# Flamingo layer on one core: transposes of y and h, and of two of four key blocks, by VectorE turns and DMA moves instead of TensorE

## The reference

```python
x = x + tanh(g_xattn) * xattn(layernorm(x), ctx, ctx, Wq, Wk, Wv, Wo, bo, g)
x = x + tanh(g_ffn) * ffn(layernorm(x), A, B, Wr)

# xattn, per batch; 8 heads of 64; the softmax of k runs over the 1024 positions, that of q over a head's 64 channels
qh = softmax(Wq @ q, over channels) * 64**-0.5
kh = softmax(Wk @ k, over positions)
context = einsum('hdn,hen->hde', kh, Wv @ v)
out = Wo @ einsum('hde,hdn->hen', context, qh) + bo
out = out / norm(out, over channels) * g * sqrt(128)

# ffn: 64 experts of rank 16, the top 16 of each token
gates = softmax(top16(x @ Wr.T)), 0 for the others
out = ((x @ A.T) * gates) @ B.T * 2
```

## Time and profile before

| | |
|---|---|
| median of 3 runs | 960.5 us (959.32 to 960.53) |
| profiled execution | 959.67 us, span of its instructions 957.9 us |
| TensorE busy | 932.2 us, 97% of the span |
| VectorE / ScalarE / GpSimd busy | 704.0 / 492.2 / 469.5 us |
| mean granted TensorE clock | 0.994 |
| stage one, rounds | context product to context product about 33 us, 16 batches |
| stage two, rounds | 24.8 us, 16 batches |

### The profile page before, as it was taken

How to read it: one execution, slowest core, us unless ns; L and a number is a source line. 1 busy time by engine, 2 the same in 40 slices (tenths; PEclk the granted TensorE clock), 3 DMA queues, 4 the chain that set the end, 5 groups by cost and what they waited for, 6 DMA issues and landing times.

```text
span 957.9 us, 16074 instructions
## 1 busy us (share of the span) xinstructions
PE 932.2 (97%) x5084; PEld 800.5 (84%) x5084; DVE 704.0 (73%) x1532; ACT 492.2 (51%) x974; POOL 469.5 (49%) x323
## 2 busy tenths in 40 slices
PE   7899999999999999999999799999999999999998
PEld 5687887888888888888888699999999999999986
DVE  6888888888888888888888857766666666666521
ACT  4687786678768767876787634222222222222100
POOL 3775657678777877785787824222222111111100
PEclk9999999999999999999999999999999999999999
DMA  4226231231323113311312853121111111111001
GB/s 153 89 66 249 93 104 49 89 133 66 109 91 133 66 68 132 109 68 66 131 45 88 300 199 128 67 67 67 66 67 67 66 66 66 66 66 45 23 23 44
DMA packets 24805, 88.31 MB, mean 92 GB/s; under 512 B 3264, under 2 KB 3264, under 8 KB 24768
## 3 DMA queue, kind: packets, MB, share of 16 engines
q1 hardware_dynamic: 19296, 67.91, 19.9%
q0 software_dynamic: 5184, 19.40, 6.1%
q10 hardware_dynamic: 288, 0.52, 0.2%
HBM read 71.04 MB, written 16.78 MB: 92 GB/s over the span
## 4 chain that ended last, share of the span: by engine, by line
PE 81%; DVE 10%; issue 5%; ACT 1%; POOL 1%; DMA 1%; DVEq 0%; ACTq 0%; POOLq 0%
PE ps L61 22%; PE ps L63 22%; PE ps L62 22%; PE ps L1307 6%; PE ps L1298 4%; DVE qT_lo L909 3%; PE ps L1288 2%; PE ps L1402 1%; PE ps L1373 1%; DVE mt L933 1%; DVE ekT_lo L916 1%; DVE qmax L895 1%; DVE bn L831 1%; DVE kmax L889 1%; DVE qsum L900 1%
## 5 line engine op out<-in xcount | busy, mean ns | idle before, releaser
L471 POOL TENSOR_TENSOR rb<-u_in,rb 128x1024 f32<-128x1024 f32 x14 | 33.7, 2408 | 255.4 <-DVE rb L885 255.4
L400 POOL TENSOR_TENSOR qe<-qe,qrec 128x1024 f32<-128x1024 f32 x64 | 121.2, 1903 | 47.1 <-DVE qrec L903 47.1
L61 PE MATMUL ps<-aT_hi,yT_hi 128*128 128x448 f32 (+2 forms) x384 | 128.4, 334 | 5.4 <-issue 5.4
L63 PE MATMUL ps<-aT_lo,yT_hi 128*128 128x448 f32 (+2 forms) x384 | 126.6, 330 | 0.0
L62 PE MATMUL ps<-aT_hi,yT_lo 128*128 128x448 f32 (+2 forms) x384 | 126.5, 330 | 0.0
L909 DVE TENSOR_TENSOR qT_lo<-ps,qT_hi 128x512 fp32r<-128x512 f32 x128 | 82.4, 686 | 49.0 <-ACT qT_hi L628 48.5
L393 POOL TENSOR_TENSOR qhalf<-qe 128x512 f32<-128x512 f32 x64 | 82.2, 1284 | 64.8 <-ACT qe L620 61.8
L61 PE MATMUL ps<-bT_hi,hT_hi 128*128 128x512 f32 x256 | 102.6, 401 | 0.0
L63 PE MATMUL ps<-bT_lo,hT_hi 128*128 128x512 f32 x256 | 100.0, 391 | 0.0
L62 PE MATMUL ps<-bT_hi,hT_lo 128*128 128x512 f32 x256 | 99.8, 390 | 0.0
L700 ACT ACTIVATE hT_hi<-ps 128x512 fp32r<-128x512 f32 x32 | 19.1, 597 | 143.8 <-PE ps L1402 143.8
(11 more groups left out here) (155 smaller groups left out, 2397.5 us busy)
## 6 DMA issues: line engine op xcount, KB each, us to landing
x_in<-in_x SPq DMA_DIRECT2D x16, 512.0 KB, 4.4
ctx_in<-in_ctx SPq DMA_DIRECT2D x16, 512.0 KB, 4.9
ctxT_in<-in_ctxT SPq DMA_DIRECT2D x16, 512.0 KB, 3.4
ctxT_hi<-in_ctxT POOLq DMA_DIRECT2D x16, 512.0 KB, 3.8
u_scratch<-osb SPq DMA_DIRECT2D x16, 512.0 KB, 3.8
out<-res SPq DMA_DIRECT2D x16, 512.0 KB, 2.8
x<-in_x SPq DMA_DIRECT2D x15, 512.0 KB, 4.0
u_in<-u_scratch SPq DMA_DIRECT2D x14, 512.0 KB, 3.2
```

The source lines that it names most:

```text
L61: nc.tensor.matmul(psum, whi, mhi, start=start, stop=False)
L63: return nc.tensor.matmul(psum, whi, mlo, start=False, stop=stop)
L400: nc.gpsimd.tensor_tensor(v, v, w, ALU.mult).then_inc(q_norm, 1)
```

## The change

Where it no longer uses TensorE, a transpose of a 128 x 1024 block takes three steps: VectorE transposes each 32 x 32 square in place (`turn_k`, `turn_y`, `turn_h`), SyncE issues 16 DMAs of 32 partitions x 256 columns that put strips of 32 columns into the partitions that they belong to (`move_turned`), and the high and low parts are made from the moved copy in SBUF (`hi_moved_*`, `lo_moved_*`).

- Stage two: y of batches 2 to 15 and h of all batches. `tr_h` is gone, `down` runs as one piece behind `up` of the next batch. A and B are laid out on the host so that rows fit the strips. y of batches 0 and 1 stays with TensorE.
- Stage one: key blocks 0 and 1. Blocks 2 and 3 stay with TensorE. `exp_k` of blocks 0 and 1 writes in strip order. Block 0 is turned in place, block 1 into a buffer of its own. The low part is made by GpSimd (`lo_moved_k`).
- The fourth query pair is normalised by ScalarE in 16 pieces of 64 columns (`normalise_q`) instead of by GpSimd.
- GpSimd's order: `normalise(b-1, 2)` goes ahead of `halve(b-1, 3)`, `halve(b, 1)` ahead of `lo_ctx(b+1, ...)`, the two `lo_moved_k` are added.
- SyncE: the loads of A go into the loop, one a round, instead of eight in a row; the moves stand behind the load of ctx and ahead of that of x.

```diff
+        def move_turned(queue, dst, src, s, slot=None):
+            for a in range(P // 32):
+                for q in range(P // 32):
+                    rows, cols = slice(32 * a, 32 * a + 32), slice(256 * q, 256 * q + 256)
+                    queue.dma_start(dst[32 * q:32 * q + 32, 256 * a:256 * a + 256],
+                                    src[rows, cols] if slot is None else src[rows, slot, cols]).then_inc(s, 16)
...
# SyncE
+            def move_k(b, j):
+                if j == 0 and started(b):
+                    wait_apart(sp, sp_turns, (kc_mm, b))
+                wait_apart(sp, sp_turns, (k_turned, turned_before(b, j) + 1))
...
                     load(ctx_in[:, :], ctx, b + 1, ctx_loaded)
+                    for j in TURNED:
+                        move_k(b, j)
...
+                if not isinstance(i, int) or b <= NB - 2:
+                    sp.wait_ge(y_turned, b)
+                    move_turned(sp, y_raw, y[(j + 2) % 2], y_moved)
                 if not isinstance(i, int) or b <= NB - 4:
-                    sp.wait_ge(y_T, 2 * b + 4)
+                    sp.wait_ge(y_moved, MOVED * b)
                     load_u(b + 3, j % 2)
+                sp.wait_ge(h_turned, b + 1)
+                move_turned(sp, h_raw, hg, h_moved)
# GpSimd
+            def lo_moved_k(b, j):
+                pool.wait_ge(k_hi, 8 * b + 2 * j + 2)
...
+                nc.gpsimd.tensor_tensor(lo, ekT_raw[j][:, :], hi.bitcast(f32), ALU.subtract).then_inc(k_lo_pool, 1)
# ScalarE
+            def hi_moved_k(b, j):
+                act.wait_ge(k_moved[j], MOVED * (b + 1))
+                nc.scalar.activation(..., ekT_raw[j][:, :], ACT.Copy).then_inc(k_hi, 2)
+            def normalise_q(b, p):
+                act.wait_ge(q_rec, 4 * b + p + 1)
+                for n in range(2 * H):
+                    v = qe[:, p, DH * n:DH * n + DH]
+                    last = nc.scalar.activation(v, v, ACT.Copy, scale=qrec[:, p, n:n + 1])
...
                     hi_kc(b - 1)
+                    normalise_q(b - 1, 3)
...
-                    hi_k(b, 0)
+                    hi_moved_k(b, 0)
+                if tail and head:
+                    hi_q(b - 1, 2)
+                if head:
                     exp_k(b, 2)
                     exp_q(b, 1)
-                if tail and head:
-                    hi_q(b - 1, 2)
# VectorE
+            def turn_k(b, j):
+                dve.wait_ge(k_exp, 4 * b + j + 1)
+                nc.vector.transpose(ek[:, 0, :] if j == 0 else ek_turned[:, :], ek[:, j % 2, :]).then_inc(k_turned, 1)
...
                     sum_q(b - 1, 2)
+                if head:
+                    turn_k(b, 0)
...
                     max_k(b, 2)
-                    lo_k(b, 0)
+                    turn_k(b, 1)
# stage two on VectorE
                     result(b - 2, ...)
+                    lo_moved_h(b - 1)
                     part_u(b + 2)
+                    turn_y(b + 1, j % 2)
                 route(b)
-                lo_h(b - 1, 1)
                     norm_u(b + 2)
                     gated(b, p)
-                    lo_y(b + 1)
-                lo_h(b, 0)
+                turn_h(b)
+                    lo_moved_y(b + 1)
                     stats2(b + 2, ...)
# TensorE, stage two
                 up(b, 0)
-                    tr_h(b - 1, 1)
+                    sum_u(b + 2)
                 up(b, 1)
                 up(b, 2)
-                    sum_u(b + 2)
-                    tr_y(b + 1, j % 2)
-                down(b - 1, 0)
-                tr_h(b, 0)
-                down(b - 1, 1)
+                down(b - 1)
```

More of the change, by code:

```diff
@@ L198, in flamingo_layer @@
             sem("k_mm"), sem("k_max"), sem("k_exp"), sem("k_T"), sem("k_hi"), sem("k_lo"), sem("k_rec"))
+        k_turned, k_moved, k_lo_pool = sem("k_turned"), [sem(f"k_moved{j}") for j in range(CH)], sem("k_lo_pool")
         q_mm, q_max, q_shift, q_exp, q_half, q_sum, q_rec, q_norm, q_T, q_hi, q_lo = (
@@ L293, in _ @@
             sp.wait_ge(wq_low, 1)
-            for t in range(DC):
-                sp.dma_start(a_raw[:, t, :], AT[t]).then_inc(a_loaded, 16)
-            with sp.Fori(2, NB - 2) as b:
+            with sp.Fori(2, 2 + DC) as b:
+                sp.dma_start(a_raw[:, bass.ds(b - 2, 1), :].rearrange("p o n -> p (o n)"),
+                             AT[bass.ds(b - 2, 1)].rearrange("o p n -> (o p) n")).then_inc(a_loaded, 16)
+                body(b, head=True, tail=True, ahead=True)
+            with sp.Fori(2 + DC, NB - 2) as b:
                 body(b, head=True, tail=True, ahead=True)
@@ L534, in _ @@
             pool.sem_inc(a_low, 1)
-            with pool.Fori(SPLIT, SPLIT + DC) as b:
+            cast_a(0)
+            with pool.Fori(SPLIT, SPLIT + DC - 1) as b:
                 body(b, head=True, tail=True, ahead=True, split=True)
+            body(SPLIT + DC - 1, head=True, tail=True, ahead=True, split=True)
             with pool.Fori(SPLIT + DC, NB - 2) as b:
@@ L1392, in up @@
                 last.then_inc(h_mm, 1)
-            def tr_h(b, g):
-                pe.wait_ge(hg_done, 3 * b + 2 + g)
-                if g == 1 or started(b):
-                    pe.wait_ge(h_lo, 2 * b + g)
-                else:
-                    pe.wait_ge(o_out, 2 * NB)
-                for n in range(4):
-                    w = (4 * g + n) * P
-                    last = nc.tensor.transpose(psG[:, n * P:n * P + P], hg[:, w:w + P], ident[:, :])
-                last.then_inc(h_T, 1)
@@ L1405, in down @@
-            def down(b, part_):
-                pe.wait_ge(h_lo, 2 * b + part_ + 1)
-                for g in range(2):
-                    if part_ == 0 and started(b):
-                        pe.wait_ge(res_done, 2 * b - 2 + g + 1)
-                    elif part_ == 0 and g == 0:
-                        pe.wait_ge(o_out, 2 * NB)
-                    v = slice(512 * g, 512 * g + 512)
-                    for m in range(KC // 2 * part_, KC // 2 * (part_ + 1)):
-                        if not started(b) and g == 0:
-                            wait_weight(pe, m)
-                        last = three_pass(psF[:, g, :], hT[0][:, m, :], hT[1][:, m, :], bT[0][:, m, v],
-                                          bT[1][:, m, v], m == 0, m == KC - 1)
-                    if part_ == 1:
-                        last.then_inc(f_mm, 1)
+            def down(b):
+                hi, lo = hT_last if isinstance(b, int) and b == NB - 1 else hT
+                first = isinstance(b, int) and b == 0
+                pe.wait_ge(h_lo, 2 * b + 2)
+                for strips in (range(KC // 2), range(KC // 2, KC)) if first else (range(KC),):
+                    for g in range(2):
+                        if first:
+                            pe.wait_ge(o_out, 2 * NB)
+                        else:
+                            pe.wait_ge(res_done, 2 * b - 2 + g + 1)
+                        v = slice(512 * g, 512 * g + 512)
+                        for m in strips:
+                            if first and g == 0:
+                                wait_weight(pe, m)
+                            last = three_pass(psF[:, g, :], hi[:, m, :], lo[:, m, :], bT[0][:, m, v],
+                                              bT[1][:, m, v], m == 0, m == KC - 1)
+                        if strips[-1] == KC - 1:
+                            last.then_inc(f_mm, 1)
@@ L1448, in body @@
                     mm_k(b, 2)
-                    tr_k(b, 0, next(turn))
                 if tail and head:
+                    tr_q(b - 1, 2, next(turn))
                     output(b - 1, 0, range(CH // 2))
@@ L1458, in body @@
                         up(0, 0)
-                    tr_q(b - 1, 2, next(turn))
-                    if not head:
+                        tr_q(b - 1, 2, next(turn))
                         output(b - 1, 0, range(CH))
@@ L1464, in body @@
                     mm_q(b, 2)
-                    tr_k(b, 1, next(turn))
                 if tail and head:
@@ L1550, in folded, with strips @@
         return w.reshape(-1, p, w.shape[1]).transpose(1, 0, 2).reshape(p, -1)
+    def strips(w):
+        return w.reshape(p // 32, -1, 32, w.shape[1]).transpose(1, 0, 2, 3).reshape(-1, p, w.shape[1])
     laid = {
```

208 lines of the change are left out of this document (136 added, 72 removed).

## The result

| | before | after |
|---|---|---|
| median | 960.5 us | 1152.0 us (4 runs, 1149.2 to 1158.1) |
| ratio | | 1.200, 95% interval 1.196 to 1.205 |
| span of the profiled execution | 957.9 us | 1149.8 us |
| TensorE busy, share of the span | 932.2 us, 97% | 961.5 us, 84% |
| mean granted TensorE clock | 0.994 | 0.926 |

What follows compares the result with a forecast made beforehand. TensorE was taken to bound both stages, VectorE close behind in stage one. Profiled 959.7 us + 44 (stage one) + 4 (first batch) + 1 (entry) + 1.3 (end) - 26.8 (stage two) = 983, forecast 984 us; range 934 to 1012.

Steps and rivals of the forecast that it cites:

- What bounds the kernel: Both stages: TensorE sets the time, busy 32.69 of 32.90 us in stage one with VectorE close behind, 24.77 in stage two.
- the chain that was named: Stage one: VectorE's turn of key block 1, SyncE's move, ScalarE's copy delay key block 2's transposes; +2.9 us a round.
- chain (b): Stage two, SyncE alone: move y, reload, move h, plus 5.9 us between; 21.9 us, fitting under TensorE's 22.96.
- X: Time of one move, first issue until all 16 DMAs landed: 8.0 us, ends 6.3 and 9.9.
- steps 1 to 5: Stage one, from VectorE's key block 0 turn to TensorE's key block 2 transposes: round 35.8 instead of 32.9, some +44 us.
- rival C: Stage one: TensorE's clock falls after idle gaps, adding 13 to 25 us: 1000 to 1010 us; chance 0.13.
- Key block 0 at no cost up to X = 8.5: Stage one: key block 0's earlier move lands about when ScalarE is ready for it, so costs nothing.
- Other work beside: Stage one: 16 ScalarE scalings, about 3.4 us, and extra GpSimd work lie beside the chain; taken as nothing.
- First batch, entry, end: Outside the regular rounds: first batch +4 us for half a move, entry to stage two +1, last batch's h +1.3.
- Stage two, -26.8: Stage two: removing 14 y blocks and 32 half blocks of h from TensorE saves 26.8 us.
- A: Rival: moves are cheap, stage one changes 0 to -10 us; 931 us, 953 at X = 6; chance 0.23.
- D: Rival: issues queue, X near 9.9, stage one +28, stage two 30 more; 1015 to 1040 us; chance 0.05.

Runs made afterwards that it cites:

- e6: The kernel before with only the change's stage-two half, SyncE and ScalarE each issuing eight of a move's 16 DMAs: 945.7 us, ratio 0.986.
- e4: The changed kernel with each move made as 4 straight DMAs of 128 partitions instead of 16, leaving out the partition exchange: 969.6 us, ratio 1.010.

## Why the prediction was wrong, point by point

**What bounds the kernel**: right. Stage one's loss came through the chain that was named, VectorE, SyncE, ScalarE, and stage two's through the chain (b).

**The price of a move**: this is the step that failed first and cost most. X was 8.0 with ends 6.3 and 9.9; it is 11.4. The landing was right (1.7 taken, 1.8 to 1.9 measured). The issue was not: 0.63, above the upper end of 0.47. Both rows behind it, four loads in 1.84 us and one at 0.33, have one end in DRAM. The trace had no DMA of that shape, as the text said; but what counted was that it had no DMA of that kind, from SBUF to SBUF, and that was not said. The upper end was therefore no bound. In stage one 3.3 us a round follow from it, some 50. In stage two the chain is 28.3 and no longer stays under TensorE's 23.06: the 14 rounds take 388.2 us where e6, with cheaper moves, takes 322.8, which is 65. It isn't the only step: at X = 8.2 the kernel took 1029.2, still above the 1012 at which the range ended.

**Stage one, steps 1 to 5**: the arithmetic holds. At X = 8.2 every mark lies within 0.2 us of what the steps give there. What it lacked was rival C, and the mistake was to hold it as a rival: it is no alternative to the waits but comes with them. The text left it out because the gaps are shorter than the one of 5.6 us in the trace; stops of 2.3 to 3.6 us were followed by the lower clock too, though not each of them. (The rule on idle gaps that the text names stands in that page of the Trainium skill under "Why this matters for your kernels".) Its price was right, 1.7 us a round forecast, 1.8 measured. With 14 of the 15 rounds of after that is 25 us, an estimate: a kernel without any slow stretch wasn't run.

**Key block 0 at no cost up to X = 8.5**: right in its consequence and at the edge of its condition. With X = 11.4 ScalarE waits 3.29 for it and TensorE 2.94 ahead of key block 3, but the wait for key block 1 behind it absorbs this, even where a slow stretch follows, as in the rounds of 225.96 to 307.32.

**Other work beside, "I take nothing"**: wrong. Scalings and order cost 10.7 us alone. Sixteen scalings take 3.9 us where 3.4 were taken. At 0.3 apiece the text named about 1 us a round, 15 in all; one took 0.333, and 8.0 us in all were found. That GpSimd has room was read off one regular round; batch 14, with its extra steps, has none, 6.3 us in the four-DMA kernel. Under the long moves these terms seem to be hidden, as after's rounds add up without them.

**First batch, entry, end**: +12.2, +6.4, +3.0 where 4, 1 and 1.3 were taken. The first batch pays about a whole move, not half of one: it was +3.2 at X = 4.0, +6.7 at 8.2, +12.2 at 11.4. At the entry TensorE waits 8.14 us for the whole of the first h, where before it could begin with a half, and the move of that h took 13.0 us instead of 11.4, beside the loads of B. Stage two alone has 4.8 us more at the entry, e6 still 2.7.

**Stage two, -26.8**: where issuing was cheap the 14 rounds gave back 16.3 us (e6) and 18.2 (e4), not 25.3, which 14 times 1.81 would be. A round without transposes is 23.06 and not 22.96 (the rows give 0.91 + 2 x 0.44 = 1.79 to take off, not 1.81); most of the rest goes in the first round, 21.9 instead of 19.5, and in the last two of the 14, which before take 23.4 and 23.8 and gave back 1.0 together in e6.

**The rivals**: A put the turning point to "faster" at X = 6.5. At X = 4.0 the kernel is still slower, 969.6 against the 931 to 953 of that case. Its regular rounds of stage one were nearly right, 32.2 to 33.1 forecast and 33.2 measured; A falls with the entry, batch 14 and the smaller gift of stage two. D described the mechanism, moves that queue and chain (b) beyond TensorE, and stopped at X = 9.9. C came with it, not in its place. That the sign was right is in part luck: the terms that were taken at nothing would have made the kernel slower even at the X of A.

The miss of 168 us adds up: 50 and 65 from the issue price in the rounds, 25 from the clock, 10 that stage two would not have given back even with cheap moves (312 us forecast for its 14 rounds, 322.8 in e6), 8 in the first batch, 5 at the entry, 2 at the end, 3 left, which is what the irregular rounds have, 168 together.

## What to carry to other kernels

Ask of every new DMA which row of the trace has the same two ends, SBUF or DRAM, and not only the same shape; where there is none, the dearest row of another kind is no upper bound, and a chain that is multiplied by 15 issues should be priced with a wide one. When an operation on the critical engine is replaced by many small transfers, the number of issues per queue decides: halve it with a second queue, or go through DRAM with five DMAs instead of sixteen. And a wait that a change puts ahead of TensorE in every round costs its own length and, more often than not here, a slow stretch behind it; the two belong in one sum.
